# TensorE's program of each local batch filled to 2,560 instructions, repeated waits left out, five orders laid out anew

## What is computed

```python
h = _layernorm(x) * (1 + ca) + sa
x = x + ga * _L0_attn_ref(h, Wq, Wk, Wv, Wo, bo)      # causal attention
h = _layernorm(x) * (1 + cb) + sb
x = x + gb * _L0_ffn_ref(h, ...)                      # the six local layers

for i in range(DEPTH):                                # DEPTH = 6, inside _L0_ffn_ref
    x = attn_layer(shift_tokens(x), Wqkv[i], q_scale[i], k_scale[i], Wo[i]) + x
    x = ffn_layer(shift_tokens(x), ln_g[i], ln_b[i], W1[i], b1[i], W2[i], b2[i]) + x
```

## Time and profile before

| | |
|---|---|
| median of 3 runs | 3508.06 us (3505.7 to 3515.55) |
| profiled execution: span from its first to its last instruction | 3495.1 us |
| what lies around the span, by the median of the runs | 13 us |
| busy in the span: PE, DVE, ACT, POOL | 95%, 84%, 71%, 83% |
| matmuls and weight loads | 69988 each |
| granted TensorE clock, mean | 0.986 of 2.4 GHz |

### The profile page before, as it was taken

One profiled execution on the slowest core, in us unless ns is written; L12 is line 12 of the kernel. 1 busy time (PEld: TensorE's weight loads), 2 busy tenths in 40 slices (PEclk: granted clock), 3 DMA queues, 4 the chain that ended last, 5 costly groups with the idle time before them and its releaser, 6 DMA issues.

```text
span 3495.1 us, 158019 instructions
## 1 busy us (share of the span) xinstructions
PE 3309.7 (95%) x69988; PEld 1936.2 (55%) x69988; DVE 2951.4 (84%) x3104; ACT 2468.4 (71%) x3349; POOL 2907.1 (83%) x2483
## 2 busy tenths in 40 slices
PE   7999999779999999999999999999999999999997
PEld 4666666445555555555555555555555555555553
DVE  6888888688888988888888889888998889988873
ACT  5777777556777767777677777676877777767764
POOL 3665555588999989999899999898999999989993
PEclk9999999999999999999999999999999999999997
DMA  1000000154645545545455454555554554545452
GB/s 67 5 5 5 5 5 5 44 119 102 143 114 130 120 115 126 131 112 127 113 126 127 106 137 110 129 120 121 120 135 105 142 124 109 140 108 134 102 124 62
DMA packets 163861, 347.33 MB, mean 99 GB/s; under 512 B 32876, under 2 KB 42352, under 8 KB 153840
## 3 DMA queue, kind: packets, MB, share of 16 engines
q1 hardware_dynamic: 163184, 337.23, 40.9%
HBM read 24.62 MB, written 4.19 MB: 8 GB/s over the span
## 4 chain that ended last, share of the span: by engine, by line
PE 70%; DVE 11%; POOL 6%; issue 6%; ACT 4%; SPq 2%; DMA 1%; DVEq 0%; POOLq 0%; ACTq 0%
PE psA L697 29%; PE psB L697 23%; PE psB L559 8%; PE psA L559 6%; PE psB L754 3%; DVE h L1338 3%; DVE pt L1237 1%; SPq L490 1%; PE psA L754 1%; DVE negm L1342 1%; DVE sum L1349 1%; DVE ts L1330 1%; DVE h L1320 1%; DMA kf<-h 1%; POOL sq L1443 1%
## 5 line engine op out<-in xcount | busy, mean ns | idle before, releaser
L1410 POOL TENSOR_TENSOR pt<-wk,pt 128x256 f16<-128x256 f32 (+3 forms) x256 | 368.1, 1455 | 288.7 <-ACT pt L939 199.0
L1443 POOL TENSOR_TENSOR sq<-sq 128x512 f32<-128x512 f32 x384 | 488.5, 1281 | 79.6 <-ACT sq L1022 78.2
L1438 POOL TENSOR_TENSOR h<-h,ts 128x512 f32<-128x512 f32 x384 | 499.8, 1302 | 1.2 <-DVE ts L1330 1.2
L1439 POOL TENSOR_TENSOR h<-h,ts 128x512 f32<-128x512 f32 x384 | 497.1, 1295 | 0.0
L1338 DVE TENSOR_TENSOR h<-h,psB 128x1024 f32<-128x1024 f32 x288 | 337.8, 1215 | 57.1 <-PE psB L697 55.5
L1463 POOL TENSOR_TENSOR pb<-pb,rc 128x1024 f32<-128x1024 f32 x192 | 366.3, 1908 | 8.8 <-DVE rc L1351 8.8
L1320 DVE TENSOR_TENSOR h<-psA,t_rot 128x1024 f32<-128x1024 f32 x192 | 234.2, 1220 | 72.7 <-ACT sq L1022 65.7
L697 PE MATMUL psA<-kf,qf 64*32 64x64 f32 x18432 | 251.2, 224 | 22.0 <-issue 21.6
L697 PEld LDWEIGHTS psA<-kf,qf 64*32 64x32 f32 x18432 | 191.5, 106 | 124.8 <-issue 124.4
L1320 DVE TENSOR_TENSOR h<-psB,t_rot 128x1024 f32<-128x1024 f32 x192 | 233.4, 1216 | 26.2 <-ACT sq L1022 20.4
L1022 ACT ACTIVATE sq<-psA 128x1024 f32<-128x1024 f32 x192 | 197.0, 1027 | 63.7 <-PE psA L697 63.5
(11 more groups left out here) (368 smaller groups left out, 10242.0 us busy)
## 6 DMA issues: line engine op xcount, KB each, us to landing
qf<-h SPq DMA_DIRECT2D x768, 136.0 KB
kf<-h SPq DMA_DIRECT2D x768, 136.0 KB, 2.5
vev<-vo SPq DMA_DIRECT2D x288, 256.0 KB
vev<-vo SPq DMA_DIRECT2D x96, 192.0 KB
stage<-wqk SPq DMA_DIRECT2D x24, 256.0 KB, 5.0
stage<-wvl SPq DMA_DIRECT2D x12, 256.0 KB, 4.1
stage<-wof SPq DMA_DIRECT2D x12, 256.0 KB, 5.5
xb<-xt SPq DMA_DIRECT2D x8, 256.0 KB, 7.9
```

The lines of the kernel that those rows point to most:

```text
L1410: e.tensor_tensor(pt[g][pr][:, :, 1, o:o + w], wk[(slot_of(s)[0] - 1) % SLOTS][:, :, 0:w], pt[g][pr][:, :, 0, o:o + w], ALU.subtract).then ...
L1438: e.tensor_tensor(halves_of(h, 0), halves_of(h, 0), t[1], ALU.subtract)
L1439: e.tensor_tensor(halves_of(h, 1), halves_of(h, 1), t[0], ALU.add).then_inc(ended["ad"])
L1443: e.tensor_tensor(sqb[c][:, 0, :], sqb[c][:, 0, :], sqb[c][:, 1, :], ALU.add).then_inc(ended["qa"])
```

## The change

Two things are added to TensorE's local program, and the five orders are exchanged. `need` takes the place of `e.wait_ge`: it leaves a wait out when this engine has already waited for that semaphore with that count or a higher one. `issued` counts the instructions since the local part's start, beginning at `LEAD` = 118: four for a float32 matmul (it runs in two passes, each a weight load and a matmul), two for others and for a transpose, and one for every two waits. After `lb` of each batch the program adds `e.sem_inc(s_pace)`, an increment of a semaphore that nobody waits for, until the count is a multiple of `BLOCK` = 256. `take` waits for the later one of `tc` and `ts` (or of `lq` and `lw`) instead of always for `ts` (`lw`). The computation is the same.

```diff
 TENSOR = (
-    "pv000:B+1 ng10+1 pv001+1 ss1:Dl+1 sc110:A+1 tp01:C+1 sc113+1 sc111+1 sc112+1 pj00:B+2 pv010:D+1 ng11+1 pv011+1 "
-    "vp10:C+1 fo:Bl tp10:C+1 vp11:A+1 bc11:B+1 bc10:C+1 f2:D+1 f0:A+1 pv100:C+1 pv101+1 pj01:D+2 tp11:B+1 pj02:A+2 "
-    "pj03:C+2 pv110:B+1 f1:D+1 pv111+1 sc000:A+2 ss0:Dl+2 sc002+2 sc001+2 pj10:D+2 sc003+2 op:Bl+1 sc010:C+2 bc00:D+2 "
-    "ng00+2 vp01:B+2 sc012+2 sc013+2 sc011+2 bc01:D+2 la:Br+2 pj11:A+2 ng01+2 pj12:B+2 vp00:D+2 tp00:C+2 sc100:A+2 "
-    "pj13:D+2 sc102+2 sc103+2 sc101+2 lb:C+2 "
+    "pv111+2 ss0:Al+3 pj10:D+3 sc000:A+3 sc001+3 sc002+3 sc003+3 op:Br+2 ng00+3 sc010:C+3 bc00:D+3 sc013+3 sc012+3 "
+    "sc011+3 vp01:A+3 ng01+3 la:Bl+3 bc01:D+3 pj11:A+3 vp00:C+3 pj12:B+3 tp00:C+3 sc100:D+3 sc101+3 sc102+3 sc103+3 "
+    "lb:C+3 pj13:A+3 pv000:B+3 ng10+3 pv001+3 tp01:C+3 ss1:Dl+3 sc110:A+3 sc111+3 sc113+3 sc112+3 fo:Br+2 pj00:D+4 ng11+3 "
+    "pv010:C+3 pv011+3 vp10:A+3 vp11:B+3 tp10:A+3 bc10:C+3 bc11:B+3 f2:D+3 f0:A+3 pv100:C+3 pv101+3 pj01:D+4 tp11:B+3 "
+    "pj02:A+4 pj03:C+4 pv110:B+3 f1:D+3 "
 )
 SCALAR = (
-    "ns1 te01 sq00+1 wh12 ex11 fh oe01 ca1 ve10 cb1 te10 ve11 ge2 ge0 oe10 sq01+1 te11 gh0 sq02+1 sq03+1 wh11+1 ge1 "
-    "tb0+2 oe11 nr0+1 ns0+1 sq10+1 tb1+2 ca0+1 cb0+1 gh1 gh2 tb3+2 ex00+1 ve01+1 oh1 tb2+2 oh0 lq+1 lw+1 sq11+1 "
-    "ex01+1 sq12+1 ve00+1 xh+2 wh02+1 te00+1 sq13+1 wh01+2 wh10+1 lr+1 ex10+1 oe00+1 nr1+1 wh00+2 "
+    "oe10+2 xh+3 wh01+3 sq01+3 wh10+3 te11+2 sq02+3 sq03+3 ge1+2 gh0+2 oe11+2 nr0+3 ns0+3 tb0+4 sq10+3 ca0+3 tb1+4 cb0+3 "
+    "gh1+2 ex00+3 tb3+4 tb2+4 ve01+3 ex01+3 lq+3 lw+3 sq11+3 ve00+3 sq12+3 wh02+3 te00+3 lr+3 sq13+3 ex10+3 oh0+2 wh12+3 "
+    "oe00+3 te01+3 nr1+3 wh00+4 wh11+3 ns1+3 sq00+4 ex11+3 ca1+3 fh+3 oe01+3 cb1+3 ve10+3 ve11+3 te10+3 ge2+3 ge0+3 gh2+3 "
+    "oh1+2 "
 )
 VECTOR = (
-    "bm01+2 sm00+2 mx01+2 bm02+2 bm03+2 tc11+2 ts11+2 tc12+2 sm01+2 ts12+2 mx10+2 tc13+2 ts13+2 wl01+3 ln+2 wl10+2 "
-    "ol00+2 sm10+2 mx11+2 wl02+2 tc00+3 ts00+3 sm11+2 ol01+2 fr+1 ow1+1 wl11+2 bm10+2 bm11+2 bm12+2 fm2+2 ws0 bm13+2 "
-    "fm0+2 wl00+3 ow0+1 ol10+2 tc01+3 ts01+3 tc02+3 ts02+3 fm1+2 ol11+2 tc03+3 wl12+2 wf0+1 wf1+1 ws1 ts03+3 mx00+3 "
-    "tc10+3 ts10+3 rs+2 bm00+3 "
+    "wl12+2 tc10+3 ws1 ts10+3 rs+2 bm00+3 mx01+3 bm01+3 sm00+3 bm02+3 bm03+3 tc11+3 ts11+3 tc12+3 ts12+3 sm01+3 mx10+3 "
+    "ln+3 ts13+3 tc13+3 ol00+3 sm10+3 wl00+4 mx11+3 wl02+3 ow0+2 wl11+3 ws0+1 fr+2 tc00+4 ts00+4 ol01+3 sm11+3 bm10+3 "
+    "bm11+3 fm2+3 bm13+3 bm12+3 fm0+3 ol10+3 tc01+4 ts01+4 ow1+2 ts02+4 tc02+4 fm1+3 wl01+4 tc03+4 ol11+3 wf0+2 ts03+4 "
+    "wf1+2 mx00+4 wl10+4 "
 )
 GPSIMD = (
-    "gl1 lx+1 nw1+1 pn10+1 cs1+1 fl+1 ct1+1 xl+2 ad13+1 pn11+1 qa00+2 ad00+2 qa01+2 qa02+2 qa03+2 ad01+2 ad02+2 gl0+1 "
-    "nw0+2 cs0+2 ct0+2 ad03+2 qa10+2 ad10+2 pn00+2 qa11+2 qa12+2 ad11+2 pn01+2 qa13+2 ad12+2 gl2+1 "
+    "gl2+2 ad00+3 xl+3 qa01+3 qa02+3 qa03+3 ad01+3 ad02+3 nw0+3 cs0+3 gl0+2 ct0+3 qa10+3 ad03+3 ad10+3 gl1+2 pn00+3 "
+    "qa11+3 ad11+3 qa12+3 pn01+3 qa13+3 ad12+3 lx+3 nw1+3 pn10+3 cs1+3 qa00+4 ct1+3 fl+3 ad13+3 pn11+3 "
 )
 SYNC = (
-    "st6 st7 dm00+1 dm01+1 dm02+1 dm03+1 st5+1 vd0+1 dm10+1 dm11+1 st4+2 dm12+1 dm13+1 vd1+1 "
+    "st6+3 dm10+3 dm11+3 dm12+3 st7+3 dm13+3 vd1+3 dm00+4 st4+4 dm01+4 st5+4 dm03+4 dm02+4 vd0+4 "
 )
...
-LAST = {"tp": "te", "op": "rs", "pj": "ts", "ss": "nr", "vp": "ve", "la": "lw",
-        "lb": "ln", "f": "fm", "fo": "fr"}
+LAST = {"tp": "te", "op": "rs", "ss": "nr", "vp": "ve", "lb": "ln", "f": "fm", "fo": "fr"}
...
+BLOCK, LEAD = 256, 118
...
         def local_tensor(e):
+            at_block, waited, open_waits = [LEAD], {}, [0]
+
+            def need(semaphore, value):
+                if waited.get(semaphore.name, 0) < value:
+                    waited[semaphore.name] = value
+                    open_waits[0] += 1
+                    e.wait_ge(semaphore, value)
+
+            def issued(n):
+                at_block[0] += n + open_waits[0] // 2
+                open_waits[0] = 0
+
             def mm(o, l, r, start=True, stop=True, **kw):
+                issued(4 if r.dtype == F32 else 2)
                 return e.matmul(o, l, r, start=start, stop=stop, skip_group_check=True, **kw)
 
             def take(s):
@@ -701,13 +722,17 @@
                 for before in place[s][1]:
                     k, at = before[0], before[1:]
                     if k == "bc":
-                        e.wait_ge(*all_done("bm", *((at[0], 2 * at[1] + x) for x in range(2))))
+                        need(*all_done("bm", *((at[0], 2 * at[1] + x) for x in range(2))))
                     elif k == "sc":
-                        e.wait_ge(*done("ex", *at[:2]))
+                        need(*done("ex", *at[:2]))
                     elif k == "pv":
-                        e.wait_ge(*done("ol", *at[:2]))
+                        need(*done("ol", *at[:2]))
+                    elif k == "pj":
+                        need(*done(*later(vector_walk, ("tc", *at), ("ts", *at))))
+                    elif k == "la":
+                        need(*done(*later(scalar_walk, ("lq", *at), ("lw", *at))))
                     else:
-                        e.wait_ge(*done(LAST[k], *at))
+                        need(*done(LAST[k], *at))
                 return psum(s)
...
                         for t in range(NT):
                             at = 512 * x + 128 * t
+                            issued(2)
                             p = e.transpose(o[:, at:at + 128], pbs[rp][:, x, t, :], ident)
...
                     p.then_inc(ended["lb"])
+                    while at_block[0] % BLOCK:
+                        e.sem_inc(s_pace)
+                        issued(1)
```

More of the change, by code:

```diff
@@ L353, in program @@
         s_masks, s_pads, s_chain, s_silu, s_mod, s_actc, s_z, s_y = (sem("s_" + n) for n in ("masks", "pads", "chain", "silu", "mod", "actc", "z", "y"))
+        s_pace = sem("s_pace")
         s_lnq, s_lnl, s_lnr, s_lnn = (sems("s_" + n, 2) for n in ("lnq", "lnl", "lnr", "lnn"))
@@ L417, in done, with later @@
             return ended[kind], count[(kind,) + at] * (64 if kind == "vd" else 1)
+        def later(steps, a, b):
+            return max(a, b, key=steps.index)
         def all_done(kind, *ats):
@@ L719, in local_tensor @@
                         for c in range(2 * rp, 2 * rp + 2):
-                            e.wait_ge(*placed(v, c))
+                            need(*placed(v, c))
                         for m, (at, n) in enumerate(((0, 1), (64, 7))):
@@ L741, in local_tensor @@
                     o = psum(("sc", v, rp, 0))
-                    e.wait_ge(*done("mx", v, rp))
+                    need(*done("mx", v, rp))
                     for x in range(2):
@@ L749, in local_tensor @@
                     o = take(s)
-                    e.wait_ge(*done("pn", v, rp))
+                    need(*done("pn", v, rp))
                     for x in range(2):
@@ L759, in local_tensor @@
                         o = take(s)
-                        e.wait_ge(*done("vd", v))
-                        e.wait_ge(*done("te", v, rp))
+                        need(*done("vd", v))
+                        need(*done("te", v, rp))
                     o = psum(("pv", v, rp, 0))
@@ L775, in local_tensor @@
                     o = take(s)
-                    e.wait_ge(*all_done("ol", *((2 * v + hf, rp) for hf in range(2) for rp in range(2))))
+                    need(*all_done("ol", *((2 * v + hf, rp) for hf in range(2) for rp in range(2))))
                     if v % NB == 0:
-                        e.wait_ge(*all_done("ow", (v - 1, 0), (v - 1, 1)))
+                        need(*all_done("ow", (v - 1, 0), (v - 1, 1)))
                     for i in range(8):
@@ L789, in local_tensor @@
                     o = take(s)
-                    e.wait_ge(*done("xl", v // 2))
+                    need(*done("xl", v // 2))
                     if b == 0:
-                        e.wait_ge(*done("wl", v // 2 - 1, half, c // 2))
+                        need(*done("wl", v // 2 - 1, half, c // 2))
                     x = [xs[b % 2][z][:, :] for z in range(2)]
@@ L806, in local_tensor @@
                     o = take(s)
-                    e.wait_ge(*all_done("qa", *((v, c) for c in range(4))))
+                    need(*all_done("qa", *((v, c) for c in range(4))))
                     for b in range(2):
@@ L815, in local_tensor @@
                     o = take(s)
-                    e.wait_ge(*done("ct", v))
+                    need(*done("ct", v))
                     for b in range(2):
@@ L825, in local_tensor @@
                     o = take(s)
-                    e.wait_ge(*done("xl", v // 2))
+                    need(*done("xl", v // 2))
                     if b == 0:
-                        e.wait_ge(*done("wl", v // 2 - 1, half, 2))
+                        need(*done("wl", v // 2 - 1, half, 2))
                     for c in range(2):
@@ L835, in local_tensor @@
                     o = take(s)
-                    e.wait_ge(*done("rs", v))
```

(15 more changed lines are left out.)

## The result

The changed kernel takes 3784.5 us (median of 4 runs) against 3511.81 us for the kernel before in the same rounds: 1.077 times as long, 95% interval 1.074 to 1.080, 273 us slower. The forecast of 3545 us had the direction and missed the size: its range ended at 3595.

What follows compares the result with a forecast made beforehand. TensorE was taken to bound the kernel. Steady batches +37 us, layers' first batches -8 and ends +8 made +37 on a span of 3495.1; with 13 us from span to median, 3545 us, range 3435 to 3595.

Steps and rivals of the forecast that it cites:

- Filling: After lb in each batch: 32 increments at 0.105 us, 3.4 us, less 1.05 us covered by lb, leave TensorE idle 2.3 us.
- Where blocks end: Code blocks of 256 instructions on TensorE, fixed by LEAD: late blocks stall it 1.8 us in every batch, bounds 0.2 and 3.
- the other two places: Short code blocks from late pv001 to sc111 and from pv111 to sc002: stalls of 0.4 us and nothing.
- Order of TensorE: Score steps stand in five runs instead of nine: 1.2 us a batch saved.
- 0.3 us for a run: Cost of each unbroken run of score steps on TensorE beyond its steps; four fewer runs were to save 1.2 us.
- the other engines' orders ... nothing: Same steps in new order on the other engines: busy times stay below TensorE's, no cost counted.
- Waits left out: 20 of 38 standalone waits a batch go from TensorE's queue: 0.1 us saved, bounds 0 and 2 us.
- The steady batch: Sum for a batch: 54.4 - 1.3 + 2.3 + 1.8 = 57.2 us against 56.3, times 41 = +37 us.
- all the ends: Extra fill in the first batch and the last two, partly covered by idle time or other engines: +8 us.
- From span to median: Last step of the sum: 13 us between span and median of the runs, added to 3532 us to give 3545.
- The layout pays: Rival: cheap or hidden increments and blocks ending where LEAD says; 3404 to 3479 us, middle 3440; chance 0.31.
- A late transfer takes over: Rival: VectorE 0.5 us later than counted makes sc100 wait for dm01's transfers; 3592 us at 1 us a batch; chance 0.13.

Runs made afterwards that it cites:

- e2: The changed kernel with LEAD = 156 in place of 118, so that a block ends with the last increment: 3731.3 us, ratio 1.063 to the kernel before.
- e14: e9 with the blocks' ends 12 instructions earlier: 3430.2 us, ratio 0.978 to the kernel before.
- e1: The changed kernel without the increments; new orders and left-out waits stay: 3509.0 us, ratio 1.001 to the kernel before.
- e3: The changed kernel with the five old orders and no increments, so only the left-out waits remain: 3492.3 us, ratio 0.996 to the kernel before.
- e5: e2 with as many increments, spread between op's wide matmuls instead of all behind lb: 3520.3 us, ratio 1.005 to the kernel before.
- e12: Like e5, increments among op's matmuls, but the blocks' ends moved to a place meant to avoid SyncE's vev burst: 3503.2 us, ratio 1.000.
- e9: e1 filled by splitting 16 of the 18 matmuls of pj11, vp00 and pj12 behind la into halves: 3469.8 us, ratio 0.990.
- e4: e3 with the increments behind lb (31 in a batch) and LEAD = 156: 3727.4 us, ratio 1.062 to the kernel before.
- e16: e3 with 16 increments behind lb and 15 behind la, none behind la in a layer's first batch: 3616.5 us, ratio 1.032.

## Why the prediction was wrong, by its own steps

- **Filling, the failed step.** "32 x 0.105 = 3.4 us", less 1.05 us of cover: 2.3 us. The cover was right (PE stands still for 3.9 us of the 4.98), the price was not: an increment stands 0.16 us behind the last, not 0.105 as a wait does, so 3.9 us: 1.6 too little. The upper bound was taken from the wrong instruction.
- **A term that was missing.** No step asked what TensorE does after a pause; it stood at nothing, and no reason was given. The clock fell to half and the 3.4 us of work behind it took 1.7 us more; late in a layer it stayed down for some 14 us. Over the run the granted clock is 0.937 against 0.986, which makes (0.986 - 0.937) x 3787 = 186 us of full rate that wasn't granted; of these 47 x 0.43 x 3.9 = 79 us fell into the pauses and about 105 us onto work.
- **Where blocks end.** LEAD = 118 against the 156 counted from the earlier trace rows: right. The gap ahead of lb was forecast at 1.4 us and is 1.55; e2 took it away. It stands ahead of lb in 31 batches; in the last two of each layer and the first of the next it stands in sc103 and has 1.2 to 2.4 us. At the other two places, forecast 0.4 and 0, TensorE doesn't wait for "issue" by more than 0.2 us in the steady batch.
- **Order of TensorE.** Forecast -1.2 us a batch. Clean batches take 54.1 us in e14 against 54.4 before: 0.3. Why the "0.3 us for a run" came to so little no run isolates. Against it stand five layers' ends with up to 5 us of wait for VectorE where the kernel before has about 3, which the step "the other engines' orders ... nothing" set at zero, and more idle time at the ends of blocks. e1 against e3: +17 us.
- **Waits left out.** Forecast 0.1 us a batch, measured (3507 - 3492) / 47 = 0.3, inside its bounds, with what the moved ends of blocks did in it.
- **The steady batch.** 54.2 (a clean batch of the new orders) + 1.55 + 3.9 + 1.7 = 61.4 us, as measured, against 53.1 + 1.8 + 2.3 = 57.2 forecast. So the 4.2 us are 1.6 of price, 1.7 of clock and 1.1 of orders and waits, less 0.25 at the blocks; price and clock are 155 of the 240 us by which the forecast fell short. Of the 273 us over the kernel before, (61.4 - 56.3) x 41 = 209 are the steady batch's; the rest is in the batches late in a layer (65 to 70 us, lower clock, and ow1 in the last one) and the first (72.6 us, 10.7 more than before, where +8 was forecast for all the ends).
- **From span to median.** The 13 us added at the end don't lie around the span: in the executions listed with both, the time is 2 to 3 us above the span, and the changed kernel's profiled span, 3787.0, is above its median. The profiled execution of the kernel before was faster than its median run.
- **Rivals.** "The layout pays" was held off by the fill, but not by it alone: e1, e5 and e12, with no pause, take 3503 to 3520 us. It pays once the ends of blocks also keep clear of the burst of transfers (e14, 3430), near the rival's middle of 3440, in part by luck, since that sum held no race and a gain of the orders four times too large. "A late transfer takes over" didn't occur at sc100; transfers did matter, by holding up code.
- **The Trainium skill's rules.** The rule in the Trainium skill, Runtime: NRT & Kernel Launch, "Instruction fetch mechanics", that fetching is hidden behind the rate of issue, would have left e2 like the changed kernel and e14 like e9; each pair differs only in where the 256 instructions end, by 53 and 40 us. The rule in the Trainium skill, PSUM — Partial Sum Buffer, "Engine vs sequencer instructions", that such an instruction waits only until earlier ones are dispatched, agrees with e5: with as many increments among wide matmuls it takes 3520 us, e1 with none 3509 (15 us by the ratios).

Open: why the lower clock lasts 3.4 us in one batch and some 14 in another (the long one has a gap of 2.17 us just ahead of the pause, but no run changes that alone); and how much of the fill's price in e4 is the clock alone, since the two pauses of e16 also have twice the cover.

## What to carry to other kernels

Price an instruction that only fills by its own spacing and by the place it stands in: behind narrow matmuls it is idle time, among wide ones nearly nothing; and add what TensorE's clock costs behind a pause. Where code arrives in blocks, look where each ends: here a block of 256 narrow instructions that ran in less than about 3.9 us stalled the next, and no block should end just as another queue issues a burst. A weight conversion of 6 us ahead of the two steps that free a bank shows only once a layer; moving it past them gave the wait to the next in line.

## What the hardware showed that was not expected

- Increments on TensorE's queue are 51 ns long and stand 0.16 us apart; waits stand 0.1 us apart.
- After 4.7 us without a load the granted clock was 0.50 for 3.4 us of full work (1.2 GHz, wide matmuls 0.43 us apart); in e16, with 1.6 and 2.2 us without one, it was 1.00 over the batch.
- A fetch of code released up to 0.11 us ahead of a burst of data came over 3 us late each time, mostly 8 us, one released 0.5 us ahead after 0.6 to 1.4 us; at 0.4 us (e14) 11 of 41 were still late.
- Two matmuls of 256 columns in place of one of 512 cost next to nothing: 16 such splits in a batch that took 54.1 us (e14), where the best batches without a split took 54.1 to 54.3 (e1).
